# Score maxima of a routed attention block: one hop into the query tile instead of two through DRAM, and query loads over two steps instead of three

## What is computed

```
qkv = x @ wqkv + bqkv
qr, kr, vr = to_regions(q), to_regions(k), to_regions(v)   # 49 regions of 64 tokens
logits = einsum('brc,bsc->brs', qr.mean(2), kr.mean(2))
_, idx = top_k(logits, 4)                                   # 4 regions for each region
kg, vg = keys and values of the chosen regions              # 256 tokens
scores = einsum('brqhd,brkhd->brhqk', qh, kh) * scale       # 8 heads of 8 channels
attn = softmax(scores, axis=-1)
out = einsum('brhqk,brkhd->brqhd', attn, vh) @ wo + bo
```

## Time and profile before

| | |
|---|---|
| median of 3 runs | 5549.65 us (5525.79 to 5556.28) |
| span of the profiled execution | 5568.0 us |
| TensorE matmuls busy | 4677.0 us, 84% |
| VectorE busy | 3447.6 us, 62% |
| ScalarE busy | 3285.4 us, 59% |
| GpSimd busy | 2747.0 us, 49% |
| DMA, queue 1 (SyncE) and 10 (ScalarE) | 16.2% and 16.4% of 16 engines' span |

### The profile page before, as it was taken

One profiled execution on the slowest core, in us unless ns is written; L12 is line 12 of the kernel. 1 busy time (PEld: TensorE's weight loads), 2 busy tenths in 40 slices (PEclk: granted clock), 3 DMA queues, 4 the chain that ended last, 5 costly groups with the idle time before them and its releaser, 6 DMA issues.

```text
span 5568.0 us, 230234 instructions
## 1 busy us (share of the span) xinstructions
PE 4677.0 (84%) x68754; PEld 3217.0 (58%) x68754; DVE 3447.6 (62%) x7969; ACT 3285.4 (59%) x6282; POOL 2747.0 (49%) x9656
## 2 busy tenths in 40 slices
PE   2388888888889888888888888888888888888888
PEld 1265565656556565565656656565565656556564
DVE  2266666666666666666666666666566666667665
ACT  1156556565665656556565665656556565665656
POOL 1245455454544545445454554545455454554553
PEclk8589999998998999889989999989899999989999
DMA  1333343333333333333333423333343333323311
GB/s 53 102 98 92 83 109 76 100 77 96 102 77 98 84 95 91 82 103 80 94 83 91 111 72 103 81 96 92 79 109 79 96 81 102 100 75 102 84 40 33
DMA packets 627124, 487.33 MB, mean 88 GB/s; under 512 B 483792, under 2 KB 613968, under 8 KB 615536
## 3 DMA queue, kind: packets, MB, share of 16 engines
q10 hardware_dynamic: 335360, 205.62, 16.4%
q1 hardware_dynamic: 290416, 265.73, 16.2%
HBM read 262.38 MB, written 208.73 MB: 85 GB/s over the span
## 4 chain that ended last, share of the span: by engine, by line
PE 45%; DMA 18%; issue 10%; SPq 7%; ACT 7%; DVE 5%; DVEq 3%; POOL 2%; ACTq 2%; POOLq 1%
DMA max_d<-tr 11%; PE ps L988 9%; PE ps L1002 7%; PE ps L1019 7%; PE ps L881 4%; DMA qm<-qk_d 3%; PE ps L938 3%; DMA xin<-in_x 3%; DVEq L223 2%; DVE mx L724 2%; SPq L327 2%; PE ps L949 2%; PE ps L901 2%; ACT hid L813 2%; PE ps L974 2%
## 5 line engine op out<-in xcount | busy, mean ns | idle before, releaser
L724 DVE TENSOR_REDUCE mx<-ps 128x4 f32<-128x1024 f32 x1568 | 1921.7, 1226 | 1702.3 <-PE ps L988 1354.0
L832 ACT ACTIVATE pt<-ps 128x512 f32<-128x512 f32 x3136 | 1694.3, 592 | 869.2 <-PE ps L1002 814.4
L506 POOL COPY vg<-vs 64x64 f32 x6272 | 1526.5, 243 | 782.0 <-POOL kg L490 576.7
L988 PE MATMUL ps<-kg,qm 96*128 96x256 f32 x6272 | 1336.2, 338 | 386.6 <-DVE mx L724 127.3
L490 POOL CAST kg<-ks 96x128 fp32r x3136 | 851.0, 297 | 1511.6 <-PE ps L1002 1156.6
L988 PEld LDWEIGHTS ps<-kg,qm 96*128 96x128 f32 x6272 | 946.8, 202 | 1053.6 <-issue 889.5
L1002 PE MATMUL ps<-qm,kg 97*128 97x256 f32 x6272 | 1119.8, 301 | 178.8 <-ACT pt L832 102.3
L1019 PE MATMUL ps<-pt,vg 128*32 128x64 f32 x50176 | 1091.4, 231 | 0.0
L1002 PEld LDWEIGHTS ps<-qm,kg 97*128 97x128 f32 x6272 | 926.2, 203 | 252.2 <-ACT pt L832 164.8
L1019 PEld LDWEIGHTS ps<-pt,vg 128*32 128x32 f32 x50176 | 826.1, 115 | 224.2 <-issue 34.8
L643 DVE CAST kg<-ks 96x128 fp32r x3136 | 625.6, 241 | 126.2 <-issue 123.5
(11 more groups left out here) (109 smaller groups left out, 3866.7 us busy)
## 6 DMA issues: line engine op xcount, KB each, us to landing
qk_d<-stg SPq DMA_DIRECT2D x224, 448.0 KB
qm<-qk_d ACTq DMA_DIRECT2D x1792, 42.0 KB
ks<-qk_d ACTq DMA_DIRECT2D x96, 784.0 KB, 6.2
vs<-v_d ACTq DMA_DIRECT2D x64, 784.0 KB, 6.7
xin<-in_x SPq DMA_DIRECT2D x119, 224.0 KB
xi_d<-xi SPq DMA_DIRECT2D x112, 224.0 KB
qk_d<-stg SPq DMA_DIRECT2D x112, 224.0 KB
max_d<-tr SPq DMA_DIRECT2D x1568, 2.0 KB
```

The source lines that it names most:

```text
L506: j = pool.tensor_copy(dst.rearrange("p j (e x) -> p j e x", e=2)[:, :, :, 0:HD], vs[place(m)[0]][rows, bass.ds(region, 1), :].rearrange(" ...
L724: v.tensor_reduce(mx[h % 2][:].rearrange("p (g j e) -> p g j e", g=2, j=2)[:, :, :, 0], ps[:, 0:2, :].rearrange("p g (j k) -> p g j k", j= ...
L832: act.activation(pt[m % 2][:, c], ps[:, 2 + c, :], ACT.Exp, scale=float(HD) ** -0.5).then_inc(S["pt_ready"], 1)
L988: i = pe.matmul(ps[:, g, 256 * j:256 * j + 256], qm[c % 2][0:NP3, t, g, 2 * j:2 * j + 2, :].rearrange("p h t -> p (h t)"), kg[slot][0:NP3, ...
```

## The change

The tensor `max_d` and the semaphores `hopped` go. SyncE waits for the transpose of step h and then issues four transfers in that same step, each from four partitions of `tr` (8j, 8j+32, 8j+64, 8j+96) to 128 numbers of the row in `qm`; all four add to `row_ready` of the step's slot, whose count is now 64 a step. `tr` has seven buffers. VectorE no longer waits before the maximum; before the transpose it waits that the row of seven steps earlier has landed. In `loads` the eight query transfers stand in steps t=3 and t=4, four in each.

```diff
+ROW_DMAS = HEADS // 2
-        max_d = dram("max_d", (RING, HEADS // 2, 128))
-        tr = [sb(f"tr{i}", [128, 32]) for i in range(2)]
+        tr = [sb(f"tr{i}", [128, 32]) for i in range(RING)]
-        hopped = [sem(f"hopped{i}") for i in range(2)]
+        def row_count(p, m):
+
+            return (p * 14 + m // NW + 1) * (16 * ROW_DMAS)
...
-            if t in (3, 4, 5) and live((c + 1) * NW, kind):
+            if t in (3, 4) and live((c + 1) * NW, kind):
-                queries(eng, p + (c + 1) // 14, (c + 1) % 14, [(g, h) for g in range(NG) for h in range(HG)][(t - 3) * 3:(t - 2) * 3])
+                queries(eng, p + (c + 1) // 14, (c + 1) % 14, [(g, h) for g in range(NG) for h in range(HG)][(t - 3) * 4:(t - 2) * 4])
...
-                m = h - 1
-                if live(m, kind):
-
-                    sp.wait_ge(hopped[m % 2], (p * R + m // 2 + 1) * 16)
-                    settled(sp)
-                    sp.dma_start(qm[m // NW % 2][NP3:NP3 + 1, m % NW].rearrange("o g h t -> o (g h t)").bitcast(F32),
-                                 max_d[m % RING].rearrange("j p -> (j p)").unsqueeze(0)).then_inc(row_ready[m % RING], 16)
                 if live(h, kind):
 
                     sp.wait_ge(S["tr_ready"], T + 1)
                     settled(sp)
-                    sp.dma_start(max_d[h % RING].rearrange("j (b n) -> b j n", n=32), tr[h % 2][0:128:8, :]).then_inc(hopped[h % 2], 16)
+                    row = qm[c % 2][NP3:NP3 + 1, t].rearrange("o g h t -> o (g h t)").bitcast(F32)
+                    for j in range(HEADS // 2):
+                        sp.dma_start(row[:, 128 * j:128 * j + 128], tr[h % RING][8 * j:128:32, :]).then_inc(row_ready[h % RING], 16)
...
                     v.wait_ge(S["sm_full"], T + 1)
-                    if live(h - 2, kind):
-                        v.wait_ge(hopped[h % 2], (p * R + (h - 2) // 2 + 1) * 16)
...
                     v.wait_ge(S["mx_ready"], T + 1)
+                    if live(h - RING, kind):
+                        v.wait_ge(row_ready[h % RING], row_count(p, h - RING))
                     settled(v)
-                    v.transpose(tr[h % 2][:], mx[h % 2][:]).then_inc(S["tr_ready"], 1)
+                    v.transpose(tr[h % RING][:], mx[h % 2][:]).then_inc(S["tr_ready"], 1)
...
-                pe.wait_ge(row_ready[slot], (p * 14 + c + 1) * 16)
+                pe.wait_ge(row_ready[slot], row_count(p, m))
```

## The result

The changed kernel takes 5991.82 us (median of 4 runs, 5975.4 to 5997.15) against 5551.55 us for the kernel before in the same comparison: 1.0771 times as long, 95% interval 1.0742 to 1.0799. The forecast was 5270 us, and the range ended at 5680.

A forecast was written before the change was run, and what follows sets the result against it. It took loaded steps to be as long as a DRAM hop, with idle stretches lowering TensorE's clock. Gains of 18 us a pass, 279 us in all, took 5568 to 5289, so 5270 against the runs' median; range 5170 to 5680.

The forecast's parts named there:

- (3): SyncE's queue, preparation phase: four transfers a step instead of two, 300 ns each, 6 us a pass gained over 36 steps.
- the sum: Whole kernel: gains of 7.5 + 2 + 6 + 2.5 = 18 us a pass, 279 us in all.
- (1): Loaded stretches and steps behind them: dropping the hop through DRAM gains 7.5 us a pass, plus 2 behind the second load.
- (4): Query loads in two steps: nearly all of TensorE's 104.5 us wait goes; 2.5 us a pass added for one stretch.
- (2): VectorE: wait before the maximum dropped; the transpose's wait for the row seven steps earlier costs nothing unless SyncE lags four steps.
- 1.6 + 4d: SyncE's time per preparation step in us, d being the issue price of one new transfer: 2.8 at 300 ns.
- The floor of 2.87: Preparation phase: least us a step after the change, a little over the quiet cycle's 2.80.
- Rival C: SyncE's queue becomes the bound in the preparation phase: at 541 ns, 26 us a pass more, less 12; 5767 us, chance 0.17.
- A: Only TensorE's two direct waits for DMA are saved, 178 us, and the clock stays: 5372 us, chance 0.18.
- B: Issue price near 0.43 us: preparation 10 us a pass slower against 12 gained elsewhere; about 5520 us, chance 0.12.
- D: The change does nothing, since steps are bound by TensorE; chance 0.03.

The follow-up runs named there:

- with two transfers: The changed kernel with two of the four row transfers left out, so the maxima of four of eight heads are not carried: 5440.9 us, ratio 0.9814.
- With three transfers: The changed kernel with one of the four row transfers left out, so the maxima of two of eight heads are not carried: 5572.13 us, ratio 1.0033.

## Why the prediction was wrong

Two steps of the prediction failed: the price of an issue in (3), and the sum, which let the gains of (1) and (4) stand beside a queue that is late. In us of a pass the first is worth 21.7 (6 gained in the sum, 15.7 lost in the trace) and the second 23.7 (12 gained, 11.7 lost).

**(1) The hop through DRAM goes: right in kind, somewhat too large in size.** VectorE's wait vanished in every kernel without the hop, and the trip itself is no obstacle: with two transfers TensorE waits 1.9 us in all for the row. The kernel with two transfers shows the gain with the queue free: 7.4 us a pass in its trace (333.7 to 326.3), 96 us by the medians, where the sum had 18 us a pass. By terms, in the means of 15 passes: the loaded seven steps and those behind the first load gained 6.2 us (7.5 credited), the four steps behind the second load 0.8 (2 credited), steps 60 to 65 1.0 (2.5), the preparation steps 2.2 (6), and other steps lost 2.8. The terms were read from a single pass. That did not make the loaded ones too large: the excess of 9.6 us over the quiet steps is 12.8 in the mean. Other waits took part of the place: TensorE waits 174.3 us for the exponentials in the run with two transfers, and 218.1 in the changed kernel, against 102.3.

**(2) VectorE's new wait: right.** The row of seven steps earlier had landed; no such wait appears. What the text named as dear if SyncE lags did come, by another way: VectorE waits for SyncE's stores of the strips.

**(3) The price of an issue: the first step that failed.** The prediction drew a line by pieces between 228 and 541 ns and took 300 for four pieces. It measured 500. The upper end was in the text, with the index row at 812 as a warning on the same kind of transfer. The formula 1.6 + 4d was close: at 500 ns it gives 3.6 us a step, and the preparation steps took 125.0/36 = 3.47 in the mean. So the term of 6 us a pass gained was 15.7 us lost; the formula would have made it 20. With three transfers the same count gives 3.05, and 3.04 were measured. The floor of 2.87 was a little low: with two transfers the queue needs 2.5, and the steps took 107.1/36 = 2.98. By the same count the kernels with two, three and four transfers need 2.5, 3.05 and 3.6 us a step, and took 5441, 5572 and 5992 us.

**The sum: the second step that failed.** With 500 ns in place of 300 the prediction's own sum is 12 gained less 20 lost, 8 x 15.5 = 124 us more than before, some 5670 us. That is still 320 us under the measured time. The missing part lies outside the 36 steps to which the prediction confined the full queue. Of the 12 us of gains a pass, the 9.5 of the loaded steps and those behind them came to 2.3 (0.8 + 1.5). The 2.5 of steps 60 to 65 became a loss of 6.7, with 2.7 more in steps 66 to 69: these ten steps inherit a late queue. Steps 84 to 90 lost 4.6 (cause open). Nowhere did the prediction count that a late store holds up VectorE and ScalarE, 338 and 252 us, or that late input holds up ScalarE.

**Rival C named the mechanism and the place**, and its sign came in: TensorE's wait for the row far above 70 us (187), with SyncE almost without idle time in the preparation phase. But it gave 5767 even at 541 ns, above the price measured, since it too set 12 us a pass of gains against the loss. The chance of 0.17 that it got was too small for a price that no row had measured.

The general rule of the Trainium skill that was weighed (DMA: Bandwidth & Descriptors, Rules for kernel authors: coalesce many small transfers into one large one) pointed the right way here: four small transfers in place of two cost 7.7%. The estimate of 0.43 us an issue, worked out from the 512 cycles of the same page's section "Why a DMA increments its semaphore by 16 and not by 1", was nearer than the line: the trace has 0.50.

**(4) The query loads: right that the wait goes** (104.5 to 14.6 us), wrong that it is worth its length: 15 us alone, while TensorE's wait for the exponentials grew by 50 us.

**The rivals A, B and D.** A's number, 5372, is the nearest to the run with two transfers (5441), but not its mechanism: it had the loaded steps stay as they are, and they gained 6.2 us a pass. B had the wrong price; D is out.

## What to carry to other kernels

Count the time of a queue that only issues, step by step and in the stretch where it has most to do, and put the price of each issue from a transfer of the same form; a price between two forms is a guess, and where the sum comes out exactly at the pace of the loop, as here, the guess decides. Once that queue is late, do not keep the gains that were counted for a queue on time, and look for what else it carries: here the steps behind the full stretch lost more than half as much as the stretch itself. A long wait of an issuing engine (1621 us) is not spare time as long as what it waits for is also what sets the pace, and it can be smaller than what replaces it. Replacing a chain of two transfers by one hop pays only if it does not turn two issues into four. And where a trace holds many passes, take the terms from their mean.

## What was unexpected

The issue of a transfer that gathers partitions cost 0.50 to 0.58 us in the median for 2 to 16 strided pieces, with no rise by their number, and 0.63 for four neighbouring ones; of the row's transfers only the one piece of 2 KB from DRAM took 0.23 us. The same form takes 507 ns on ScalarE's queue, where it is dearer for the kernel: two more a step there turn 5441 us into 6304, two more on SyncE into 5992. And the cost of issues has a knee: 131 us for the third transfer of a step, 420 us for the fourth.
